# Placing a group one step earlier, and 71 expert blocks instead of 72, in a mixture-of-experts and attention kernel

## The reference

```python
logits = x @ gate_w
top_v, top_i = jax.lax.top_k(logits, K)          # K = 2
top_p = jax.nn.softmax(top_v, axis=-1)
d = (silu(x @ Wg[e]) * (x @ Wu[e])) @ Wd[e]      # for the two chosen e, inner width 352
shared = silu(x @ Sg) * (x @ Su) @ Sd            # for every token, inner width 176
```

## Time and profile before

| | us |
|---|---|
| median of 3 runs | 1247.82 (1246.77 to 1250.56) |
| profiled execution, its own time | 1248.63 |
| its span, first to last instruction | 1246.6 |
| PE busy | 999.2 (80%) |
| DVE busy | 900.7 (72%) |
| POOL busy | 846.9 (68%) |
| ACT busy | 673.8 (54%) |

### The profile page before, as it was taken

How to read it: one execution, slowest core, us unless ns; L and a number is a source line. 1 busy time by engine, 2 the same in 40 slices (tenths; PEclk the granted TensorE clock), 3 DMA queues, 4 the chain that set the end, 5 groups by cost and what they waited for, 6 DMA issues and landing times. The chain is left out here.

```text
span 1246.6 us, 32188 instructions
## 1 busy us (share of the span) xinstructions
PE 999.2 (80%) x9076; PEld 750.5 (60%) x9077; DVE 900.7 (72%) x2377; ACT 673.8 (54%) x1474; POOL 846.9 (68%) x878
## 2 busy tenths in 40 slices
PE   2667655999999937788988898888864999999940
PEld 1444334899989924455555555555433899898940
DVE  6778783666766744788888888888854666666748
ACT  5556642555555623466666555666431555555545
POOL 4677773777777844467787787878642777777850
PEclk8889986999999967999999999999976999999975
DMA  9311121222222211001111111100003222222229
GB/s 280 104 49 49 54 85 55 79 77 76 82 75 76 74 56 34 17 29 42 34 34 35 49 36 38 42 19 17 20 33 82 77 78 77 78 74 77 73 89 332
DMA packets 69023, 86.89 MB, mean 70 GB/s; under 512 B 13164, under 2 KB 56625, under 8 KB 68974
## 3 DMA queue, kind: packets, MB, share of 16 engines
q1 hardware_dynamic: 51566, 52.41, 14.5%
q0 software_dynamic: 17408, 33.87, 8.2%
HBM read 45.01 MB, written 43.30 MB: 71 GB/s over the span
## 5 line engine op out<-in xcount | busy, mean ns | idle before, releaser
L489 POOL DMA_INDIRECT expert_results<-ey,eidx x288 | 299.6, 1040 | 70.8 <-issue 64.8
L481 POOL DMA_INDIRECT routed_rows<-row,idx x256 | 253.4, 990 | 73.6 <-issue 71.1
L1128 DVE SCALAR_TENSOR_TENSOR ehT<-eh,ehT 128x768 f16<-128x768 f32 x144 | 138.0, 958 | 151.6 <-ACT ehT L681 151.6
L676 ACT ACTIVATE esil<-PSUM 128x768 f32<-128x768 f32 x144 | 116.8, 811 | 236.3 <-PE PSUM L815 226.7
L813 PE MATMUL PSUM<-eT,WGU 128*128 128x256 f16 x864 | 237.7, 275 | 1.2
L814 PE MATMUL PSUM<-eT,WGU 128*128 128x256 f16 x864 | 237.4, 275 | 0.0
L815 PE MATMUL PSUM<-eT,WGU 128*128 128x256 f16 x864 | 237.4, 275 | 0.0
L503 POOL TENSOR_TENSOR space<-qk,val 128x1152 f32<-128x1152 f32 x64 | 138.3, 2172 | 73.7 <-DVE shift L1178 52.5
L813 PE MATMUL PSUM<-WD,ehT 128*128 x864 | 164.0, 221 | 7.8 <-DVE ehT L1128 5.2
L814 PE MATMUL PSUM<-WD,ehT 128*128 x864 | 162.6, 221 | 0.1
L815 PE MATMUL PSUM<-WD,ehT 128*128 x864 | 162.1, 220 | 0.0
(11 more groups left out here) (197 smaller groups left out, 2306.2 us busy)
## 6 DMA issues: line engine op xcount, KB each, us to landing
xe<-routed_rows SPq DMA_DIRECT2D x144, 130.0 KB
space<-expert_results SPq DMA_DIRECT2D x32, 512.0 KB, 4.1
expert_results<-ey,eidx POOLq DMA_INDIRECT x288
X<-in_L_attn_x_dram SPq DMA_DIRECT2D x16, 256.0 KB, 4.7
routed_rows<-row,idx POOLq DMA_INDIRECT x256, 2.3
out_dram<-X SPq DMA_DIRECT2D x16, 256.0 KB, 4.4
routed_rows<-pad_rows SPq DMA_DIRECT2D x24, 130.0 KB
space<-in_L_ffn_Wg_dram SPq DMA_DIRECT2D x1, 1408.0 KB, 9.1
```

What stands on the lines that cost most here:

```text
L481: pool.indirect_dma_start(routed, bass.IndirectOffsetOnAxis(ap=idx[u][:, k, j:j + 1], axis=0), row[u][:, j, :], None).then_inc(s_scattered ...
L489: pool.indirect_dma_start(result, bass.IndirectOffsetOnAxis(ap=eidx[u][:, h:h + 1], axis=0), ey[u][:, h, :], None, bounds_check=K * T - 1, ...
L676: act.activation(esil[u][:, :], PSUM[:, 1536 * u:1536 * u + 768], ACT.Silu, scale=2.0 ** -(SX + SWT)).then_inc(s_block_silu, 1)
L1128: return dve.scalar_tensor_tensor(out=dst, in0=src, scalar=float(2 ** scale), in1=high, op0=ALU.mult, op1=ALU.subtract)
```

## The change

In the first stage, DVE no longer calls `place(n)` at the start of step n. It calls `place(n + 1)` in step n, behind `row_low(n + 2)` and ahead of `shared_add(n - 1)`. `place(0)` stays at the start of step 0, and `place(1)` stands in step 0 right behind `choose(1)`, ahead of `moments(1, 5)`, `row_low(2)` and `shared_low(0)`.

In both expert stages the last block (number 71) is neither loaded nor computed nor scattered. So that the counting semaphores of the second expert stage keep their values, each engine raises the semaphores of the missing block by a `drain` at its end. The waits on `s_results` count 36 blocks for the even and 35 for the odd buffer.

```diff
             def load_block(f):
                 def step(n, v):
+                    if isinstance(n, int) and n == (f + 1) * NBLK - 1:
+                        sp.wait_ge(s_block_rows[v], (n - v) * (16 // XE))
+                        sp.drain().then_inc(s_block_rows[v], 16)
+                        return
...
             def results(n, u):          # POOL
+                if isinstance(n, int) and n in (NBLK - 1, 2 * NBLK - 1):
+                    pool.drain().then_inc(s_carrier, 1)
+                    return
...
-                    pool.wait_ge(s_results[u], 16 * HALVES * NBLK // 2 * (f + 1))
+                    pool.wait_ge(s_results[u], 16 * HALVES * (NBLK // 2 - u) * (f + 1))
...
             def experts(f):             # ACT
-                with act.Fori(0, (NBLK - 4) // 2) as i:
+                with act.Fori(0, (NBLK - 6) // 2) as i:
                     step(i * 2 + (n0 + 4), 0)
                     step(i * 2 + (n0 + 5), 1)
-                hi(n1 - 1, 1)
+                step(n1 - 2, 0)
+                hi(n1 - 2, 0)
+                results(n1 - 3, 1)
                 results(n1 - 2, 0)
-                results(n1 - 1, 1)
+                act.drain().then_inc(s_block_silu, 1)
+                act.drain().then_inc(s_block_high, 1)
+                act.drain().then_inc(s_block_results, 1)
...                                      # PE
-                for m in range(2 + (NBLK - 4) // PASS * PASS, NBLK):
-                    step(m, m % XE, e, turn=m < NBLK - 1, read=m < NBLK - 1)
+                for m in range(2 + (NBLK - 4) // PASS * PASS, NBLK - 1):
+                    step(m, m % XE, e, turn=m < NBLK - 2, read=m < NBLK - 2)
+                block_down(n1 - 3, 1, e[1])
                 block_down(n1 - 2, 0, e[2])
-                block_down(n1 - 1, 1, e[3])
+                pe.drain().then_inc(s_block_turned, 1)
+                pe.drain().then_inc(s_block_products, 1)
+                pe.drain().then_inc(s_block_out, 1)
...                                      # DVE
-                step(n1 - 2, 2)
-                step(n1 - 1, 3, ahead=False)
-                block_low(n1 - 1, 1)
+                step(n1 - 2, 2, ahead=False)
+                block_low(n1 - 2, 0)
+                dve.drain().then_inc(s_block_T, 1)
...                                      # and three more like it
             def first_ffn(n, v, i=None, b=None):   # DVE
-                place(n, v, n)
                 if edge and n == 0:
+                    place(0, 0, 0)
                     deviations(3, 1, 4)
...
                 if not edge or n < NG - 1:
                     choose(n + 1, (v + 1) % 4, n + 1)
                 if edge and n == 0:
+                    place(1, 1, 1)
                     moments(1, 5)
                 if not edge or n < NG - 2:
                     row_low(n + 2, (v + 2) % 4)
+                if not edge or 0 < n < NG - 1:
+                    place(n + 1, (v + 1) % 4, n + 1)
                 if not edge or n > 0:
                     shared_add(n - 1, n - 1)
```

More of the change, by code:

```diff
@@ L411, in _ @@
                 for u in range(2):
-                    sp.wait_ge(s_results[u], 16 * HALVES * NBLK // 2 * (f + 1))
+                    sp.wait_ge(s_results[u], 16 * HALVES * (NBLK // 2 - u) * (f + 1))
                 if f == 0:
@@ L693, in res_value @@
             def res_value(n, u):
-                return (n - u) * (16 * HALVES // 2)
+                return (n - u) * (16 * HALVES // 2) - 16 * HALVES * u * ffn[0]
             def experts(f):
@@ L1311, in experts @@
                         step(i * XE + (n0 + 2 + b), (2 + b) % XE)
-                step(n1 - 2, 2)
-                step(n1 - 1, 3, ahead=False)
-                block_low(n1 - 1, 1)
+                step(n1 - 2, 2, ahead=False)
+                block_low(n1 - 2, 0)
+                dve.drain().then_inc(s_block_T, 1)
+                dve.drain().then_inc(s_block_hidden, 1)
+                dve.drain().then_inc(s_block_low, 1)
+                dve.drain().then_inc(s_block_places, 1)
             def combine_first(g):
```

## The result

The changed kernel takes 1241.61 us (median of 8 runs, 1238.33 to 1244.66), the kernel before 1248.05 in the 8 runs beside it (1246.41 to 1250.56). The ratio is 0.9948 with an interval of 0.9937 to 0.9960: 6.4 us faster, between 5.0 and 7.9. The forecast was 1238.4, a gain of 9.4 us, which is outside that interval; the number that came is that of rival 1 (1241.1). Its profiled execution took 1242.69 us with a span of 1240.9.

What follows compares the result with a forecast made beforehand. POOL's chain, started late, was taken to bound the first stage and PE the expert stages; 2.7 us from the moved `place` plus 6.68 from the blocks made 9.4, so 1247.82 - 9.4 = 1238.4 us, range 1235.5 to 1242.

Steps and rivals of the forecast that it cites:

- rival 1: First stage gains nothing: step 2's delay or 0.2 to 0.3 us more per loop step eats it; 1241.1 us, chance 0.17.
- Blocks: Expert stages: each loses one steady period, 3.34 us; two give 6.68 us, bounds 5.3 and 7.2, drains costing nothing.
- Rival 3: Expert stages: POOL's own pace sets their end, so a block is worth 2.67 us; 1239.8 us, chance 0.06.
- Steps 0 to 3 of the first stage: DVE's step 2 starts 2.05 us later, yet `idx(3)` comes at 55.9 and its ticket at 56.0, against 57.85.
- Group 7: First stage: POOL free at 98.3, `idx(7)` at 98.6, so the group starts 3.0 us earlier.
- `place` itself doesn't wait for PE: First stage, loop steps: `positions` is done at 70.75, before `row_low` ends at about 71.9.
- the forecast 0.4 at group 11: First stage: POOL free at 140.4 but `idx(11)` at 140.8, so the group starts at 140.8 instead of 143.38.
- POOL's own time from group 3 on: First stage: 42.3 us to group 7, later spans as before, 52.9 from group 11; POOL's work ends at 193.7.
- rival 2: First stage: POOL waits at neither group 7 nor 11, and collisions are fewer; gain 4.7 us, 1236.4 us, chance 0.12.
- Rival 4: First stage: PE falls to 1.2 GHz in loop steps, 1.7 us more per step; 1252.2 us, chance 0.03.
- Attention and last stage as long as before: A sign that the forecast is right: the attention stage and the last stage keep their length.

Runs made afterwards that it cites:

- b_only_2: Against the kernel before, on a fast chip: 71 blocks in each expert stage, `place` left at the start of its step; 1242.83 us, ratio 0.9963.
- p_only_2: Against the kernel before, on a fast chip: only `place` moved, still 72 blocks in each expert stage; 1246.71 us, ratio 0.9992.
- m_ticket_2: Changed kernel with POOL's ticket a memset behind a semaphore increment, on a fast chip; 1241.64 us, ratio 0.9953 to the kernel before.
- before_again: The kernel before, unchanged, profiled again on a chip where it takes 1406 us; 1407.29 us, ratio 1.0006.

## Why the prediction was right and where it failed

- **Blocks: right by the profiles, less by the times.** One steady period per stage was forecast, 6.68 us for both; the profiles with 71 blocks are 3.4 and 3.3 us shorter in these stages than those with 72. The drains cost nothing that can be seen. The times of `b_only_2` give 4.6 us with 6.0 as the upper end, under the forecast. Rival 3, 2.67 a stage, is therefore not excluded: it is under both profile values, but not by more than the stages wander.
- **Steps 0 to 3 of the first stage: right.** Group 1 began without a wait, group 2 with 1.34 us of it, group 3 at 56.22 with a wait of 4.39, all within 0.4 us of the forecast.
- **Group 7: a step that failed, but cost little.** The forecast had `idx(7)` at 98.6, and the ticket at once. It came at 99.93 + 0.22. 0.66 us of this stood ahead of it: `row_low(8)` ended at 98.43 instead of 97.77. 0.29 of that was there at `row_low(4)`, which began 2.34 us later than before (54.69 against 52.35) instead of 2.05; the rest came in the loop, where three starts of `shared` (60.11, 69.64, 79.15) are 9.52 us apart instead of 9.42. The other 0.86 is the step "`place` itself doesn't wait for PE". That was read in an ordinary step. In step 6 `positions` is queued behind everything that PE does late and slowly after the `deviations`; the row for it, `ups` at 0.65 behind an idle of 4.75, stood in the same group of rows, read for step 2 only. Yet POOL itself was not free for group 7 before 99.55, where 98.3 was forecast, so the late `idx(7)` cost a wait of 0.69 us in place of a forecast 0.3, and the forecast 0.4 at group 11 did not occur.
- **The term that was mis-sized: POOL's own time from group 3 on.** The forecast has 137.0 us of it (42.3 to group 7, 140.4 - 98.6 = 41.8 to group 11, 52.9 to the end), as in the kernel before, where it is 136.99 (196.28 - 57.85 - 1.44). It was 139.54 (196.45 - 56.22 - 0.69). With the 0.22 us by which group 3 started late, and waits of 0.69 where 0.7 were forecast, this is the whole 2.75 us by which the last DMA's end missed 193.7. 2.27 of the 2.55 us over the kernel before are the three stretched tickets. The forecast named such collisions, but only between DVE's piece and a DMA, and only fewer of them were priced, as the upper bound of the gain; more of them had no price.
- **Rival 1** gave the right number, but not by its mechanism: a loop step was 0.1 us longer, not 0.2 to 0.3, and POOL's waits behind group 3 were as forecast. What ate the gain is rival 2's mechanism, the collisions, with the other sign. That the time fell within the range, which goes up to rival 1, is to this extent luck. The range's lower end, added up again from its own terms, is 1235.9 (1247.82 - 4.7 - 7.2) and not 1235.5. Rival 4 did not come on this kind of chip: `ups` in ordinary steps kept 0.38 to 0.41 us.
- **"Attention and last stage as long as before": wrong in the profile**, by 2.1 us more in the attention stage, 2.9 of them at one place where the granted clock was 0.58 over 7 us. Sum of the profile: +0.2 - 4.1 + 2.1 - 3.9 = -5.7. As the same loss is in `p_only_2`, I don't put it down to the change. How often the kernel before has it is not known, since only one profile of it on this kind of chip exists; so nothing of it is added to or taken from the ratio.
- The Trainium skill, "SBUF — State Buffer", section "Who interferes with whom", calls the shared ports an exclusive lock: whoever comes second waits. The tickets that end 0.04 to 0.05 us behind DVE's instruction fit it, and the one at 185.85 (0.63 us) fits it in order too, having begun second. The ticket at 77.86 fits it in size: it ends at 78.99, where DVE's piece, from 78.07, ends at 78.95. But it began 0.21 us ahead of the piece, so by the rows the one that was first was held too (a profile's start times of POOL are rough, but the ticket at 121.87, 0.20 us ahead of its piece, shows the same). And the page's inference that a two-input operation of DVE leaves descriptor work alone is contradicted again, by the DMA at 77.95 of `m_ticket_2`: 1.63 us.

## What to carry to other kernels

A wait removed on the engine that sets the end is worth only what the next late input, and the engine's own time, leave of it: follow the producer's whole chain to each place where the consumer may stop, above all through the steps that differ from the ordinary one. When two engines with different periods share memory, moving one of them shifts which instruction collides; put such collisions into the range with both signs, and don't expect a cheaper instruction to end them. And take more than one profile before pricing an edit of 3 us by stages: the same code wandered by 1 to 3 us a stage.

## What was not expected of the hardware

Three chips run the same program 11 to 13% slower (1386 and twice 1406 us against 1248), and in the expert stage not by a lower clock of TensorE. PE in the window from 300 to 400 us of the kernel before, first on the fast chip and then in `before_again`:

```profile
300.00:400.00 100.00, 99.73 (x1209) 1.00 0.27 77
```

```profile
300.00:400.00 100.00, 88.52 (x980) 1.00 0.21 62
```

The clock is full in both, and `silu` takes 812 and 809 ns. What grows is the time between engines: ACT by lines in that window of `before_again`, with the releaser marked as remote that never shows in the same window on the fast chip:

```profile
L676 ACT ACTIVATE esil<-PSUM 128x768 f32<-128x768 f32 x24 | 19.4, 809 | 27.2 <-remote 18.5 <-PE PSUM L815 8.6
```

24 blocks pass in 100 us instead of 30 or 31. On the chip with 1386 us the new place alone was worth 13 us, and taking a block out was worth nothing that was measured. What lengthens the hand-overs is open; so is why `m_both`, the change with two instructions of POOL replaced by a shorter one and a semaphore instruction ahead of each, is 3% slower there.
